# Another order of the blocks of a batch: attention over a long context with a mixture of experts

## The reference

```python
q = (Q @ W_q.T) ; k = (K @ W_k.T) ; v = (V @ W_v.T)      # split into 16 heads of 8
scores = einsum('bhqd,bhkd->bhqk', q, k) / sqrt(8)
e = exp(clip(scores, -50, 50)) ; attn = e / sum(e)
x = x + (attn @ v, heads joined) @ W_o.T                 # times a mask over the tokens
```

## Time and profile before

| what | value |
|---|---|
| median of three runs | 1106.81 us |
| the profiled execution | 1106.66 us |
| its span, first to last instruction | 1104.9 us |
| mean granted TensorE clock | 0.969 |
| TensorE matmuls busy | 1033.4 us, 94% |
| ScalarE busy | 769.6 us, 70% |
| VectorE busy | 761.0 us, 69% |
| GpSimd busy | 240.0 us, 22% |
| DMA, mean | 156 GB/s |

### The profile page before, as it was taken

The page is one execution under the profiler, slowest core; times in us unless marked ns, Lnnn a source line. Parts: engine busy times, 40 slices in busy tenths (PEclk is TensorE's granted clock), DMA queues, the critical chain, the costliest instruction groups (busy, mean ns, idle before and its releaser), DMA issues.

```text
span 1104.9 us, 32396 instructions
## 1 busy us (share of the span) xinstructions
PE 1033.4 (94%) x10544; PEld 759.8 (69%) x10545; DVE 761.0 (69%) x2088; ACT 769.6 (70%) x1088; POOL 240.0 (22%) x320
## 2 busy tenths in 40 slices
PE   5789999999999999999999999999999999399990
PEld 3567677777777677777677777777767776299990
DVE  4567777777777777777777777777777777444433
ACT  2567877777777877777877777877778777144430
POOL 3331111111111111111111111111111111245554
PEclk8899999999999999999999999999999999699995
DMA  7645555455555554555455555555555544022216
GB/s 217 186 154 166 173 170 170 165 166 167 168 171 170 172 171 164 173 167 170 167 171 173 173 173 173 174 174 174 174 174 174 174 157 142 23 68 63 65 49 178
DMA packets 144319, 172.71 MB, mean 156 GB/s; under 512 B 32235, under 2 KB 88559, under 8 KB 144287
## 3 DMA queue, kind: packets, MB, share of 16 engines
q1 hardware_dynamic: 138622, 165.26, 45.4%
q0 software_dynamic: 4896, 6.63, 2.2%
q10 hardware_dynamic: 768, 0.41, 0.2%
HBM read 36.83 MB, written 22.08 MB: 53 GB/s over the span
## 4 chain that ended last, share of the span: by engine, by line
PE 90%; DMA 3%; POOL 2%; SPq 2%; DVE 1%; issue 1%; ACT 1%; ACTq 0%; POOLq 0%; DVEq 0%
PE scores L753 31%; PE o_sum L765 26%; PE scratch L687 7%; PE scratch L676 7%; PE scores L873 5%; PE scores L884 5%; PE scratch L671 4%; PE scratch L726 1%; SPq L535 1%; POOL w_sb L597 1%; PE scratch L681 1%; PE scratch L731 1%; DMA x_all<-in_x_dram 1%; DMA q_stack<-q_rep 1%; PE scratch L747 1%
## 5 line engine op out<-in xcount | busy, mean ns | idle before, releaser
L990 ACT ACTIVATE probs<-scores 128x800 f32<-128x800 f32 (+1 forms) x640 | 615.2, 975 | 160.7 <-PE scores L753 158.6
L753 PE MATMUL scores<-q_stack,k_stack 128*128 128x400 f32 x1536 | 415.2, 380 | 10.5 <-DMA q_stack<-q_rep 8.1
L1136 DVE TENSOR_SCALAR probs<-probs 128x800 f32<-128x800 f32 (+1 forms) x640 | 396.2, 654 | 25.2 <-ACT probs L990 25.0
L753 PEld LDWEIGHTS scores<-q_stack,k_stack 128*128 128x128 f32 x1536 | 249.2, 190 | 110.5 <-issue 100.9
L765 PE MATMUL o_sum<-probs,v_both 128*17 128x200 f32 x6144 | 316.3, 335 | 0.1
L765 PEld LDWEIGHTS o_sum<-probs,v_both 128*17 128x17 f32 x6144 | 151.1, 97 | 132.4 <-issue 71.9
L630 POOL DMA_INDIRECT expert_rows<-rows,row_atu x64 | 75.6, 1181 | 408.8 <-DVE row_atu L1233 361.4
L687 PE MATMUL scratch<-w_turned,ctxT 128*128 128x128 f32 x768 | 102.5, 277 | 0.0
L687 PEld LDWEIGHTS scratch<-w_turned,ctxT 128*128 128x128 f32 x768 | 101.2, 194 | 0.0
L1073 DVE COPY v_both<-scratch 128x512 f32<-128x512 f32 x93 | 64.4, 692 | 42.4 <-PE scratch L687 42.4
L1048 DVE CAST k_hi<-k_full 128x512 fp32r<-128x512 f32 (+1 forms) x93 | 38.4, 412 | 79.5 <-ACT k_full L932 79.4
(11 more groups left out here) (145 smaller groups left out, 771.1 us busy)
## 6 DMA issues: line engine op xcount, KB each, us to landing
k_stack<-k_hi SPq DMA_DIRECT2D x192, 256.0 KB, 2.5
k_stack<-k_lo SPq DMA_DIRECT2D x192, 256.0 KB, 2.6
expert_rows<-fill SPq DMA_DIRECT2D x32, 406.2 KB
xT_and_ctx<-in_ctx_dram SPq DMA_DIRECT2D x16, 704.0 KB
ctx_nat<-in_ctx_dram SPq DMA_DIRECT2D x16, 704.0 KB
q_rep<-q_parts SPq DMA_DIRECT2D x124, 50.0 KB, 1.9
q_stack<-q_rep SPq DMA_DIRECT2D x124, 50.0 KB, 1.9
v_both<-expert_rows SPq DMA_DIRECT2D x57, 65.0 KB, 1.8
```

Source lines behind the costliest of these rows:

```text
L753: last = nc.tensor.matmul(score_banks(c)[:, m, :], k_stack[p][:, g, t * P:(t + 1) * P], q_stack[p][:, :, g, :], start=True, stop=True)
L990: nc.scalar.activation(probs_of(c), score_banks(c), ACT.Exp, scale=SCALE).then_inc(exp_ready, 1)
L1136: nc.vector.tensor_scalar(chunk, chunk, LOW, HIGH, ALU.max, ALU.min).then_inc(probs_ready, 1)
```

## The change

Three tables get other numbers. Before, the chunks have 3, 2, 3, 2, 3, 2, 3, 2, 2, 2 units (twice), now 2, 2, 3, 2, 3, 2, 3, 2, 3, 2 (twice). The halves stood in nine runs of 2, 2, 2, 6, 1, 3, 2, 2 and 4, now in eight of 2, 1, 3, 4, 3, 3, 6 and 2; before, six of the halves ran in the next batch, now eight. Of the steps, turns 0 and 1 both stand in chunk 0 (before 0 and 1), the keys in chunks 10, 11, 11 (before 2, 4, 10), the values in 4, 6, 12 (before 12, 14, 17), the query in 9 (before 5); the finishing steps move by one or two chunks, and rank stays in 19.

```diff
-    UNITS = [3, 2, 3, 2, 3, 2, 3, 2, 2, 2] * 2
+    UNITS = [2, 2, 3, 2, 3, 2, 3, 2, 3, 2] * 2
...
-    HALF_AT = [5, 5, 6, 6, 8, 8] + [10] * 6 + [12, 15, 15, 15, 18, 18, 20, 20] + [22] * 4
+    HALF_AT = [7, 7, 8, 11, 11, 11, 14, 14, 14, 14, 16, 16, 16, 18, 18, 18, 21, 21, 21, 21, 21, 21, 23, 23]
...
-    STEPS = [("turn", 0), ("turn", 1), ("key", 0), ("key", 1), ("heads", 0), ("query", 0), ("queries", 0),
...
+    STEPS = [("turn", 0), ("turn", 1), ("value", 0), ("heads", 0), ("value", 1), ("queries", 0),
...
-    STEP_AT = [0, 1, 2, 4, 4, 5, 8, 8, 9, 10, 12, 12, 13, 14, 17, 19]
+    STEP_AT = [0, 0, 4, 5, 6, 7, 8, 9, 10, 10, 11, 11, 12, 14, 15, 19]
```

More of the change, by code:

```diff
@@ L110, in xattn_moe @@
     FINISH = [("heads", 0), ("queries", 0), ("project", 0), ("tokens", 0), ("gate", 0), ("rank", 0)]
-    STEPS = [("turn", 0), ("turn", 1), ("key", 0), ("key", 1), ("heads", 0), ("query", 0), ("queries", 0),
-             ("turn", 2), ("project", 0), ("key", 2), ("value", 0), ("tokens", 0), ("gate", 0), ("value", 1),
-             ("value", 2), ("rank", 0)]
-    STEP_AT = [0, 1, 2, 4, 4, 5, 8, 8, 9, 10, 12, 12, 13, 14, 17, 19]
+    STEPS = [("turn", 0), ("turn", 1), ("value", 0), ("heads", 0), ("value", 1), ("queries", 0),
+             ("project", 0), ("query", 0), ("turn", 2), ("key", 0), ("key", 1), ("key", 2),
+             ("value", 2), ("tokens", 0), ("gate", 0), ("rank", 0)]
+    STEP_AT = [0, 0, 4, 5, 6, 7, 8, 9, 10, 10, 11, 11, 12, 14, 15, 19]
     IN_LAST = [s in FINISH for s in STEPS]
```

## The result

The changed kernel takes 1090.43 us (median of four runs, 1089.8 to 1090.76), the kernel before on the same chip 1106.53: a ratio of .985, 95% interval .9835 to .987. The forecast was 1091.8, so it held; but two of its terms were wrong and cancelled, and two gains were not in it. The profiled execution has a span of 1088.6 us, against 1104.9.

What follows compares the result with a forecast made beforehand. TensorE's full string of blocks was taken to bound the kernel at 28.2 us per batch. From 1106.66 us, -.38 per batch over thirty batches (-11.4) and -3.5 in the first batch gave 1091.8, range 1087.5 to 1099.

Steps and rivals of the forecast that it cites:

- 1 runs, nine to eight: Value runs per batch: one run fewer with the halves still 24 saves one fixed cost, -.13 us.
- 3 double turn: Turns 0 and 1 standing together: turn 0 ahead of another turn takes .44 instead of .53, -.09 us per batch.
- 5 turn 2 ahead of key 0: Turn 2 with its short last tile, now followed by key 0: still .60 as ahead of a run, 0 per batch.
- 6 value 0, value 1: Value projections: 0 goes on to scores instead of tokens, -.08; 1 loses its Scalar engine wait, -.12 us per batch.
- Step 4: Key 0 goes on to scores instead of a run, -.18 us per batch; query and output projection swap such places and cancel.
- The first batch: GpSimd's normed tokens start earlier, so one TensorE wait and the lower clock go; 1 to 2 us of wait stays: -3.5 us.
- The ends: First batch does two fewer halves (-.68), they return behind the last (+.68); expert stage untouched: 0.
- bank wait at the double turn: Turn 1 waits for rank's scratch bank, freed late by the Vector engine: +24 us, 1116; chance .06.
- late keys: Key splits all in chunks 10 and 11 queue twelve transfers, keys arrive late: slower, no size given; chance .02.
- bunching of the Scalar engine: Copies bunched in chunks 0, 10 and 11 make two waits of .12 per batch: +7.2 us, 1099; chance .17.
- second fall of the clock in the first batch: A 2 us wait in chunk 8 lowers the clock again: +1.7 us, 1093.5; chance .08.
- the four rivals below 1104: Scalar bunching 1099 (.17), first batch gains nothing 1095.3 (.12), clock falls again 1093.5 (.08), cheaper seams 1086.4 (.08).

Runs made afterwards that it cites:

- e2_turns_apart: The changed kernel with turn 1 put back into chunk 1: 1094.46 us, ratio .9894 to the kernel before.
- e3_full_tile: The changed kernel with the last context tile zero-filled and transposed at its full height of 128 rows: 1082.69 us, ratio .979 to the kernel before.
- e9_query_first: The changed kernel with query and output projection exchanged, query in chunk 8 and projection in 9: 1094.01 us, ratio .9896 to the kernel before.
- e8_before_full: The kernel before with the last context tile transposed at its full height of 128 rows: 1104.73 us, ratio .9985.
- e4_early_moments: The kernel before with the first batch's late moments taken in chunks 0, 1, 3, 5 instead of 3, 4, 5, 7: 1100.19 us, ratio .9948.
- e7_after_moments: The changed kernel with the first batch's late moments taken in chunks 0, 1, 3, 5 instead of 3, 4, 5, 7: 1089.74 us.
- e13_project_later: The changed kernel with full-height last tile, halves of chunks 7 and 8 merged, early first-batch moments, and the output projection moved to chunk 9: 1078.55 us.
- e1_merge: The kernel before with the halves of chunk 5 joined to those of chunk 6, eight runs instead of nine: 1109.35 us, ratio 1.0033.
- e11_new_units: The kernel before with only the new cut into chunks, its runs and steps left as they were: 1111.92 us, ratio 1.0064.
- e12_next_order: Another order of steps with six runs, plus full-height last tile and early first-batch moments: 1098.88 us, ratio .9935 to the kernel before.
- e6_merge_7_8: The changed kernel with the halves of chunks 7 and 8 merged into one run of three behind chunk 8: 1086.69 us, ratio .9814 to the kernel before.

## Why the prediction was right, and where it was not

By its own steps, per batch:

| step | forecast | measured | by |
|---|---|---|---|
| 1 runs, nine to eight | -.13 | -.13 | their starts: 9.25 to 9.12 in all |
| 2 score groups and their ends | +.13 | +.13 | all scores, those behind key 0 put at .66: 10.67 to 10.80 |
| 3 double turn | -.09 | -.09 | .79; e2_turns_apart |
| 4 key 0 ahead of scores | -.18 | -.09 | .56 + .96 against .95 + .66; e3_full_tile |
| 4 query and projection | 0 | -.08 | .14 + .31 against .39 + .14; e9_query_first |
| 5 queries ahead of a run | +.09 | +.09 | .18 |
| 5 turn 2 ahead of key 0 | 0 | 0 | .60 |
| 6 value 0, value 1 | -.08, -.12 | -.08, -.12 | .81 each; no wait left |
| sum | -.38 | -.37 | period -.37 |

The method held: blocks priced by the distance between starts, with their neighbours, add up to the batch within .01 us. (By their two decimals the rows of the prediction give .12 for a run and .03 for a group of scores, where it has .13 and .04; this changes its sum by nothing that counts.) **Step 4 was mis-sized twice.** Key 0 was to save a whole entry (.18). It saved half, because it now follows the short tile, and the way back costs at two places: .17 in turn 2, which the prediction took (its .60 was right), and .10 more behind key 0, which it did not. The trace of before held only half of the clue: turn 2 cost .07 more than turn 0 there, ahead of a run, and the run hides the rest, as e8_before_full shows. With the full tile of e3_full_tile key 0 and its scores take 1.42, .19 less than the 1.61 of before: there the whole entry is saved. And query and projection were to cancel: as entries into a run they do (.15 and .17), but query's .39 held .10 of a wait for the Scalar engine's copy of key 1, which the prediction put at nothing (e9_query_first). The two errors, +.09 and -.08, cancel, and so 27.82 against a forecast of 27.8 says less for the steps than it seems.

**The first batch** gained 4.4 beside its two halves, not 3.5 (range 3.5 to 4.5). The mechanism is the one forecast, and e4_early_moments and e7_after_moments show it: it is GpSimd's chain. The step that was off is the wait that was to stay, 1 to 2 us for group 4: .6 stayed. GpSimd started 2.5 earlier, not 2, and needed 4.36 instead of 5.02. By the waits, 3.8 - .6 and the 1.7 of the lower clock are 4.9, less the new wait for the Vector engine, .6: 4.3. Two more things are not in that sum and work against each other: TensorE's waits for exponentials rose from .5 to 1.2 (30 to 75 us), as the prediction had expected of the two turn copies, and from 33 to 42 us the clock was higher than before (.77 against .64). They were not separated.

**The ends** were taken as 0. Last batch and tail came to +.4: the tail took .6 more, near the .68 of two halves, and the last batch .2 less. The expert stage gained .8 though nothing in it changed, and no step had that: its first wait for a transfer is followed by some 6.4 us at a lower clock instead of 7.0 (the granted clock is back at 951.9 behind a first matmul at 945.5, before at 967.9 behind one at 960.9), and one wait for a transfer is .3 shorter. At half the clock .6 us less of it is worth .3, so that these two are some .6 of the .8. It is a matter of where the stage falls, not of the order of a batch; that was read from two traces and not tested.

**The rivals.** In the trace of after TensorE has no listed wait between 100 and 900 us: no bank wait at the double turn, no late keys, no bunching of the Scalar engine; and no second fall of the clock in the first batch. But e13_project_later shows the bank wait at another pair of steps, e1_merge, e9_query_first and e11_new_units each show an exponential as the new wait, and e12_next_order the Vector engine. So these rivals were real, and the order of the change avoids them; how much room it leaves was read for the double turn alone. The chances that the prediction gives the forecast and the four rivals below 1104 add up to .91, not to its .89.

## What to carry to other kernels

Price a block by the distance from its start to the next start, with its neighbour, and a reordering of a full engine can be summed seam by seam. But each block that goes is also cover: before a seam is taken out, look up which copy, exponential or bank the next instructions wait for and how much of its time the block had hidden. And a small operand can be the dear one: where one tile of a full-height stream is short, filling it up with zeros may cost less than changing the shape twice.

## What the runs showed of the hardware

- A transposed tile of 36 rows between full-height matmuls costs .26 us more per batch than one of 128 rows (e3_full_tile); ahead of narrow products it costs .07 more (e8_before_full).
- The cost shows in part one block late: key 0 itself takes .56 behind the short tile, and the scores behind it .96; with the full tile .50 and .92.
- A wait for a copy cost more here than the lateness of the start: the projection of e6_merge_7_8, which started .05 behind the end of the copy, took .39 instead of .31 to the next start, beside the .08 that it waited. The query of the kernel before, whose weights were loaded .15 behind the end of a copy, took .39, and .29 in e9_query_first.
- Such a wait can stand under "issue" in the profile: those 28 waits of the query do.
- A busier row can be a slower one: 8.36 of 9 us with 28 matmul records at a granted clock of .50, 7.08 with 32 at .77.
